# A mixture-of-experts kernel on one core: the order of one loop over blocks of 384 rows

## The reference

```python
def cond(x, y, weight):
    ys = y * 256 ** -0.5
    d = rsqrt(einsum('bi,io->bo', ys * ys, weight * weight) + 1e-8)
    return einsum('bsi,io->bso', x * ys[:, None, :], weight) * d[:, None, :]

def ffn(z, W1, b1, W2, b2, Wr, br):
    route_w = softmax(einsum('bsd,de->bse', z, Wr) + br)
    mask = one_hot(top_k(route_w, 2)[1], 8).sum(-2)
    routed = route_w * mask
    routed = routed / routed.sum(axis=-1, keepdims=True)
    h = relu(einsum('bsd,edh->ebsh', z, W1) + b1[:, None, None, :])
    expert_out = einsum('ebsh,ehd->ebsd', h, W2) + b2[:, None, None, :]
    return einsum('bse,ebsd->bsd', routed, expert_out)

out = x + ffn(cond(x, cond_1024, L0_cond_weight), ...)
```

## Time and profile before

| | |
|---|---|
| median of 3 runs | 875.57 us (873.85 to 875.98) |
| the profiled execution, its own time | 876.02 us |
| its span, first to last instruction | 874.1 us |
| TensorE, matmuls (PE) | 847.0 us busy, 97% |
| TensorE, weight loads (PEld) | 832.0 us, 95% |
| VectorE (DVE) | 715.2 us, 82% |
| ScalarE (ACT) | 561.3 us, 64% |
| GpSimd (POOL) | 457.4 us, 52% |
| TensorE's granted clock, mean over the span | 0.993 |

### The profile page before, as it was taken

One profiled execution on the slowest core, in us unless ns is written; L12 is line 12 of the kernel. 1 busy time (PEld: TensorE's weight loads), 2 busy tenths in 40 slices (PEclk: granted clock), 3 DMA queues, 4 the chain that ended last, 5 costly groups with the idle time before them and its releaser, 6 DMA issues.

```text
span 874.1 us, 20313 instructions
## 1 busy us (share of the span) xinstructions
PE 847.0 (97%) x6248; PEld 832.0 (95%) x6248; DVE 715.2 (82%) x1418; ACT 561.3 (64%) x1005; POOL 457.4 (52%) x424
## 2 busy tenths in 40 slices
PE   7996999999999999999999999999999999999995
PEld 7975999999999999999999999999999999999995
DVE  3795888899999888788878887888788878888884
ACT  5775766688777665565656555665566566677773
POOL 6983544454544445454545454554455455565553
PEclk9998999999999999999999999999999999999998
DMA  7895847777353454435443543352352524774762
GB/s 228 304 313 185 288 94 186 201 238 202 83 147 65 95 127 95 112 45 136 91 103 49 135 101 90 49 139 55 85 99 52 139 38 115 185 201 122 208 192 25
DMA packets 55002, 118.40 MB, mean 135 GB/s; under 512 B 7312, under 2 KB 33328, under 8 KB 54320
## 3 DMA queue, kind: packets, MB, share of 16 engines
q1 hardware_dynamic: 25040, 69.48, 24.4%
q0 software_dynamic: 25536, 35.69, 23.7%
q10 hardware_dynamic: 4384, 12.71, 4.2%
HBM read 91.07 MB, written 35.17 MB: 144 GB/s over the span
## 4 chain that ended last, share of the span: by engine, by line
PE 76%; DVE 8%; ACT 7%; issue 5%; DMA 2%; ACTq 1%; DVEq 1%; POOL 0%; SPq 0%; POOLq 0%
PE psum L1680 13%; PE psum L1681 12%; PE psum L1682 12%; PE psum L1698 12%; PE psum L1697 12%; PE psum L1696 12%; ACT w_hi L792 2%; ACT h L865 2%; PE psum L1658 2%; DVE w_lo L1413 2%; DVE early_row_hot L1136 1%; DVE h_lo L1475 1%; DVE y L1443 1%; ACT h_hi L863 1%; PE psum L1570 1%
## 5 line engine op out<-in xcount | busy, mean ns | idle before, releaser
L865 ACT ACTIVATE h<-psum,b_all 128x384 f32<-128x384 f32 (+1 forms) x376 | 209.0, 559 | 229.9 <-PE psum L1682 213.3
L1696 PE MATMUL psum<-w_hi,h_hi 128*128 128x256 f32 x1056 | 296.5, 281 | 1.4 <-DVE h_lo L1475 1.4
L1698 PE MATMUL psum<-w_hi,h_lo 128*128 128x256 f32 x1056 | 295.9, 280 | 0.1
L1697 PE MATMUL psum<-w_lo,h_hi 128*128 128x256 f32 x1056 | 295.9, 280 | 0.0
L1680 PE MATMUL psum<-z_hi,w_hi 128*128 128x384 f32 (+1 forms) x752 | 251.4, 334 | 5.1 <-DVE w_lo L1413 3.1
L1413 DVE TENSOR_TENSOR w_lo<-raw,w_hi 128x1024 fp32r<-128x1024 f32 x188 | 229.4, 1221 | 22.0 <-ACT w_hi L792 21.9
L1681 PE MATMUL psum<-z_lo,w_hi 128*128 128x384 f32 (+1 forms) x752 | 245.3, 326 | 0.0
L1682 PE MATMUL psum<-z_hi,w_lo 128*128 128x384 f32 (+1 forms) x752 | 245.1, 326 | 0.0
L1475 DVE TENSOR_TENSOR h_lo<-h,h_hi 128x384 fp32r<-128x384 f32 (+1 forms) x376 | 200.9, 534 | 28.8 <-ACT h L865 14.8
L792 ACT ACTIVATE w_hi<-raw 128x1024 fp32r<-128x1024 f32 x188 | 198.6, 1057 | 10.6 <-PE psum L1698 9.7
L1696 PEld LDWEIGHTS psum<-w_hi,h_hi 128*128 128x128 f32 x1056 | 199.7, 189 | 3.1 <-issue 3.1
(11 more groups left out here) (239 smaller groups left out, 749.7 us busy)
## 6 DMA issues: line engine op xcount, KB each, us to landing
raw<-in_experts SPq DMA_DIRECT2D x96, 512.0 KB
x_buf<-in_xT SPq DMA_DIRECT2D x12, 512.0 KB, 8.8
z_rows<-z_all ACTq DMA_DIRECT2D x2, 2112.0 KB, 10.5
d_rep<-d_rows SPq DMA_DIRECT2D x3, 1056.0 KB, 6.7
z_rows<-z_all SPq DMA_DIRECT2D x1, 2112.0 KB, 12.2
z_rows<-z_once SPq DMA_DIRECT2D x1, 2112.0 KB, 15.3
raw<-in_xT SPq DMA_DIRECT2D x4, 512.0 KB, 9.6
out<-y,idx_put POOLq DMA_INDIRECT x91
```

Of the source, the lines that this page charges most:

```text
L865: act.activation(h[c % NHP][:, 0:width], h_ps[c % n_h][:, 0:width], ACT.Relu, bias=b1_all[:, ds(e, 1), c]).then_inc(s_relu, 1)
L1696: pe.matmul(yp, hi, w2(w_hi, c), start=(c == 0), stop=False)
L1697: pe.matmul(yp, hi, w2(w_lo, c), start=False, stop=False)
L1698: ins = pe.matmul(yp, lo, w2(w_hi, c), start=False, stop=(c == HC - 1))
```

## The change

In the blocks of the loop, and nowhere else, the second product runs three chunks behind the first instead of two; the next block's rows are transposed in chunk 4 instead of chunk 2; quarter 0 of the next block's weights is split in chunk 5 (ScalarE) and chunk 6 (VectorE) instead of chunk 4 on both; and quarter 1 after the z copies at the block's end instead of in chunk 5. The early blocks and the tail keep their order.

```diff
-    LAG = 2
-    LAG_WIDE = 3
+    LAG = 3
...
             def block_of_act(b, fresh, tail=False, final=False):
-                wide = tail or is_early(b)
...
-                    if c == (5 if wide else 4) and not final:
+                    if c == 5 and not final:
                         weights_hi(b + 1, 0, seg_next, False)
-                    if c == 5 and not wide:
-                        weights_hi(b + 1, 1, seg_next, False)
...
                 z_hi_of(b + 1, False, width)
-                if wide:
-                    weights_hi(b + 1, 1, seg_next, False)
+                weights_hi(b + 1, 1, seg_next, False)
...
             def block_of_dve(b, fresh, tail=False, final=False):
-                wide = tail or is_early(b)
...
-                    if c == (6 if wide else 4) and not final:
+                    if c == 6 and not final:
                         weights_lo(b + 1, 0)
-                    if c == 5 and not wide:
-                        weights_lo(b + 1, 1)
...
                 z_lo_of(b + 1, width)
-                if wide:
-                    weights_lo(b + 1, 1)
+                weights_lo(b + 1, 1)
...
             def block_of_pe(b, fresh, tail=False, final=False):
-                lag = LAG_WIDE if tail or is_early(b) else LAG
+                lag = LAG
                 for c in range(HC):
-                    if c == (4 if fresh else 4 if tail else 2) and not final:
+                    if c == (2 if is_early(b) and not fresh else 4) and not final:
                         transpose_z(b + 1, tail)
                     first_product(b, c, fresh, tail)
                     if c >= lag:
```

## The result

| | before | after |
|---|---|---|
| median | 874.68 us (873.57 to 875.98, 5 runs) | 884.15 us (883.36 to 885.74, 5 runs) |
| the profiled execution's span | 874.1 us | 883.8 us |
| one block of the loop | 17.37 us | 17.76 us |

The ratio of after to before is 1.0112, with a 95% interval from 1.0101 to 1.0123: the change makes the kernel 9.5 us slower by the medians, 8.8 to 10.8 us by the interval. The forecast was 885.8 us, in a range of 883 to 889. It stood on the median of three runs of before, 875.57 us; the five runs of the table have 874.68, so 0.9 of the 1.65 us between forecast and measurement are a lower starting point, and the rest is the size of the loss.

What follows compares the result with a forecast made beforehand. TensorE, busy 97% of the span, was taken to bound the kernel. A new wait of 11.0 us less 0.7 us gained made +10.3 us: 886.3 us from the profiled execution, 885.8 us against the median, range 883 to 889.

Steps and rivals of the forecast that it cites:

- the loop had nothing to give: Loop: TensorE has almost no idle time, so the new order can give at most 0.03 us per block, 0.7 us.
- the early blocks' 17.34 us: Length of one undisturbed early block, already in the order "three behind", against 17.36 us for a loop block.
- F3: First product of chunk 3 in a loop block; claimed to wait for relu 1, costing 0.46 us per block, 11.0 us.
- rival A: Loop: not slower, blocks at the early blocks' pace of 17.34 us, 874.9 us; chance 0.08.
- The three terms: Fourth first product of a loop block: 0.30 late, 0.05 relu to start, 0.11 blocked start; sum 0.46 us per block.
- its better floor: Loop blocks: the new order gives at most about 0.03 us per block, 0.7 us in 24 blocks.
- F4: First product of chunk 4 in a loop block; claimed to have some 0.4 us to spare for quarter 2's low half.
- The short way of the wait: Loop, relu 1 to the waiting product: 0.05 us, since the wait hangs on the matmul; 0.13 us kept as upper end.
- The parts costed at nothing: Loop: weights converted later, and z_lo, w_lo, y, r_cur in a row at the block's end; all covered, no cost.
- that leaves some 0.4 us: Loop, first product of chunk 4: wanted near 6.15 us into the block, its weights ready at 5.65, or 5.78.
- B: Loop: a second wait, at chunk 4's first product, for VectorE's quarter 2; 4 to 7 us more, 890 to 893; chance 0.05.
- The rival of the clock: Loop: TensorE's clock falls to 1.2 GHz for one product per block; 22 us more, 907 us; chance 0.01.

Runs made afterwards that it cites:

- the last run: The change plus relu 1 ahead of quarter 2, three buffers in the loop, and the tail's quarter 3 one chunk earlier; ratio 0.9915, 868.53 against 876.04... us.
- the lag alone: The kernel before with only the second product three chunks behind in the loop; ratio 1.0128, medians 887.24 and 875.38 us.
- one line in the tail: Against the kernel before, VectorE splits quarter 3 behind chunk 2 instead of 3 in the tail; run alone, ratio 0.9956, 870.50 and 875.03 us.
- the split quarter: The change, with ScalarE's conversion of quarter 2 in the loop made in two halves ahead of relu 1; ratio 1.0133, 886.21 and 875.03 us.

## Why the prediction was right, point by point

**That the loop had nothing to give.** TensorE was idle for 0.1 us in it. The best order tried takes 17.31 us per block, 0.06 under before. The forecast took the early blocks' 17.34 us as the floor, 0.03 too high, which is under 1 us in all.

**The place and the cause.** F3 waits for relu 1, once per block, 24 times; 3.47 us behind F0, as worked out. Five runs take away one condition each (transposes ahead of F3, in chunk 2 or 3; relu 1 ahead of the conversion; a third buffer; S0 ahead of F3, with the transposes alone in chunk 4), and each removes this wait; one makes the relu later, and the block grows by as much. So it takes all four together: four first products in a row, two buffers, a conversion between two relus, and no transposes ahead. The words of rival A, that in the early blocks this order "runs without a wait", hold for the undisturbed block of the earlier trace rows only; the earlier trace rows are of an early block that did wait.

**The size.** The three terms, 0.30 late, 0.05 from relu to product, 0.11 for the blocked start, measured 3.42 - 3.12 = 0.30, 0.05 and 0.11. 17.76 is 0.45 us above the 17.31 that this order of TensorE takes without a wait in the loop (the last run). The term that was mis-sized is the small one: the forecast gave the new order 0.03 us per block for its better floor, and it was 0.06. It lies at F4: before, S1 ahead of F4 takes 1.05 us (514.01 to 515.06) and F4 1.07 (to 516.13), where second and first products in the middle of the last run's block take 1.02 and 1.05; why is not shown. So the block grew by 0.39 and not by 0.43 us, 9.4 instead of 10.3 us in 24 blocks; the times alone, with 8.8 to 10.8 us, would not tell the two apart. Two small slips of the sum changed nothing: 875.57 + 10.3 is 885.9, and the upper end of the range, 875.6 + 13.0, leaves out the 0.7 us that the lower end takes off.

**The short way of the wait.** The choice between 0.05 and 0.13 us was made by where the wait hangs in the order of instructions. It holds: waits on the matmul itself (F3, and S6 with the lag alone) cost 0.05 us, waits on a register instruction ahead of it (F4 for its weights, S0) 0.13 and 0.14 us, both inside the loop. The 0.13 of the earlier trace rows, which the prediction calls "inside the loop", had been read in the tail.

**The parts costed at nothing.** The later weights are free (0.9998). In the block of after, VectorE's row of the quarter at the end of the block, r_cur and quarter 2:

```profile
511.14 1.22 DVE L1408 TENSOR_TENSOR w_lo<-raw,w_hi 128x1024 fp32r<-128x1024 f32 x1
...
513.64 0.17 DVE L1445 COPY r_cur<-r_next 128x3 f32<-128x3 f32 x1
...
517.15 1.22 DVE L1408 TENSOR_TENSOR w_lo<-raw,w_hi 128x1024 fp32r<-128x1024 f32 x1
```

The quarter ends at 512.36, 0.4 us ahead of F0; r_cur is taken 0.9 us behind F0, quarter 2 ends at 518.37, 5.63 us behind F0, and F4 at 6.11 has time. But the sentence "that leaves some 0.4 us" for F4 was true only as long as F3 waited. This is where a rival was underrated: B, a second wait at F4, did not come in the change, but it came in two of the five runs that cured F3 (transposes back in chunk 2, three buffers), and there it took back some 0.12 us of the 0.45 that the cure had won.

**What the prediction did not ask** is what each part is for. The lag of three without the later weights is worse than the whole change (17.87 us). The rival of the clock did not come: the digits stayed at 9 in the loop with 24 small stalls, each of 0.35 us, one in 17.8 us. The Trainium skill (TensorE: Matmul & The Clock Gate, section "A second HAM failure mode: psum-queue depth-cycling") tells of another kernel whose clock swung with small idles between its groups of matmuls; the stalls of this case did not bring that about.

## What to carry to other kernels

When an order is copied from one stage of a kernel to another, compare not the order but what stood ahead of each wait in the stage where it works: here 0.46 us of transposes (or the second product that a lag of two puts there) were the cover, and the new order took it away. An engine without idle time turns every 0.1 us of lateness into time, so check each first use (buffer, weights, operand) for its margin, and after curing one wait expect the next one within the same 0.3 us. And look for stalls where the profile shows them, rather than in the stage that is dense: one line in the tail was worth three times what the best order tried gave in the loop (4.2 against 1.4 us).

## What the runs showed of the hardware

**A start that is on time can still cost 0.08 us.** F2 of the change starts at its wanted time, 514.82, but its second matmul comes 0.25 us later instead of 0.17. The weight loads of the same moments (start, length) tell why:

```profile
514.47 0.19 PEld L1673 LDWEIGHTS psum<-z_hi,w_lo 128*128 128x128 f32 x1
514.79 0.19 PEld L1671 LDWEIGHTS psum<-z_hi,w_hi 128*128 128x128 f32 x1
...
515.08 0.19 PEld L1673 LDWEIGHTS psum<-z_hi,w_lo 128*128 128x128 f32 x1
...
516.21 0.19 PEld L1671 LDWEIGHTS psum<-z_hi,w_hi 128*128 128x128 f32 x1 [0.42 <-ACT h L863]
```

The load at 514.47 belongs to a matmul that starts at 514.64, 0.17 us later; F2's load should have started at 514.65, but relu 0 ended at 514.16 + 0.58 = 514.74, and the load stands at 514.79. A late load does not always cost: with the relu ahead of quarter 2, F3's load starts at 513.43, 0.11 us ahead of its matmul (513.54) instead of 0.17, because relu 1 ended only 0.16 us ahead, and the next matmul still follows after 0.17 us. In all three cases the second matmul starts 0.28 us behind the first load: 513.71 - 513.43, 515.07 - 514.79, 516.49 - 516.21. So for these products a relu that ends 0.16 us ahead of the matmul costs nothing, one that ends 0.08 us ahead costs 0.08, and one that the matmul waits for costs 0.11 on top of the wait. The Trainium skill (TensorE: Matmul & The Clock Gate, section "Step-by-step: what each phase is for") has weight loads pulled ahead of matmuls in flight. The trace agrees where nothing waits: loads start 0.17 us ahead of their matmuls. At F3 the load starts with the end of the wait, and the row of the wait is the load's own ([0.42 <-ACT h L863]); whether a load would pass a matmul that alone is held up is not shown here. This small price appears at F2 wherever no transposes stand ahead of it and the buffers are two, at S0 too with the transposes alone in chunk 4, and nowhere in the loop of the last run but behind the transposes.

**A wait on a register instruction ahead of the matmul** is released some 0.08 us later than one on the matmul: 0.13 us (F4 with the transposes back in chunk 2 and with three buffers) and 0.14 (S0) against 0.05 (F3 in the change and with the split quarter, S6 with the lag alone). It is not a matter of which engine is waited for: S6 waits for VectorE, as F4 and S0 do. The register instruction itself has a row of 0.03 us in the trace, from 515.59 for the F4 that starts at 515.68.
